# A Macaron block with an S4D layer: 14 other token orders in the square layers, and the last matrix moved by 64 bytes

## The reference

```python
def _L0_ffn_ref(x, w1_w, w1_s, w2_w, w2_s, h1_w, h1_s, h2_w, h2_s, w3_w, w3_s):
    h = jax.nn.silu(_tlin(x, w1_w, w1_s)) * _tlin(x, w2_w, w2_s)   # 256 -> 1024
    h = jax.nn.gelu(_tlin(h, h1_w, h1_s), approximate=False)       # 1024 -> 1024
    h = jax.nn.gelu(_tlin(h, h2_w, h2_s), approximate=False)       # 1024 -> 1024
    return _tlin(h, w3_w, w3_s)                                    # 1024 -> 256

x = x + 0.5 * _L0_ffn_ref(_layernorm(x, axis=-1), ...)
x = x + _L0_attn_ref(_layernorm(x, axis=-1), ...)    # FFT convolution with the S4D kernel, gelu, 256 x 256 projection
x = x + 0.5 * _L0_ffn_ref(_layernorm(x, axis=-1), ...)
```

## Time and profile before

| | |
|---|---|
| median of 2 runs | 1431.37 us (1431.02 to 1431.71) |
| the profiled execution, its own time | 1433.21 us |
| span of its trace, from the first to the last instruction | 1431.4 us |
| TensorE (PE) busy | 1423.7 us, 99% |
| VectorE (DVE) busy | 986.3 us, 69% |
| ScalarE (ACT) busy | 477.7 us, 33% |
| granted TensorE clock | 1.000 |

### The profile page before, as it was taken

One profiled execution on the slowest core, in us unless ns is written; L12 is line 12 of the kernel. 1 busy time (PEld: TensorE's weight loads), 2 busy tenths in 40 slices (PEclk: granted clock), 3 DMA queues, 4 the chain that ended last, 5 costly groups with the idle time before them and its releaser, 6 DMA issues.

```text
span 1431.4 us, 17284 instructions
## 1 busy us (share of the span) xinstructions
PE 1423.7 (99%) x6918; PEld 1166.7 (82%) x6918; DVE 986.3 (69%) x1736; ACT 477.7 (33%) x724; POOL 48.1 (3%) x42
## 2 busy tenths in 40 slices
PE   9999999999999999999999999999999999999998
PEld 4788888888878888788787888878878788888887
DVE  7867867775778887848878587784777754453433
ACT  5524342433425124232242332422424223141321
POOL 0000000000000000010000100001000010000000
PEclk9999999999999999999999999999999999999999
DMA  9000000011113211131210312112120212010000
GB/s 369 16 0 30 30 30 30 16 45 59 42 65 127 74 60 59 32 112 46 87 60 12 133 45 74 34 41 99 60 74 15 59 44 71 1 45 0 30 1 16
DMA packets 53906, 80.28 MB, mean 56 GB/s; under 512 B 2752, under 2 KB 45632, under 8 KB 52544
## 3 DMA queue, kind: packets, MB, share of 16 engines
q1 hardware_dynamic: 53824, 79.15, 16.3%
HBM read 57.12 MB, written 22.02 MB: 55 GB/s over the span
## 4 chain that ended last, share of the span: by engine, by line
PE 98%; DVE 1%; ACT 0%; issue 0%; POOL 0%
PE ps L1327 80%; PE ps L1403 8%; PE ps L1454 3%; PE ps L1507 2%; PE ps L1303 1%; PE ps L1449 1%; PE ps L1448 1%; PE ps L1416 1%; PE ps L1387 1%; PE ps L1497 0%; PE ps L1320 0%; PE ps L1389 0%; DVE hid_b_lo L1221 0%; PE ps L1431 0%; PE ps L1439 0%; DVE hid_b_hi L1219 0%
## 5 line engine op out<-in xcount | busy, mean ns | idle before, releaser
L503 ACT ACTIVATE act_o<-ps,scales 128x512 f32<-128x512 f32 x384 | 264.5, 690 | 897.1 <-PE ps L1327 895.3
L1327 PE MATMUL ps<-hid_b_hi,h 128*128 128x512 f32 x1024 | 401.5, 392 | 0.5 <-DVE hid_b_lo L1221 0.5
L1327 PE MATMUL ps<-hid_b_lo,h 128*128 128x512 f32 x1024 | 398.7, 389 | 0.0
L1327 PE MATMUL ps<-hid_a_hi,h 128*128 128x512 f32 x992 | 390.1, 393 | 0.1
L1327 PE MATMUL ps<-hid_a_lo,h 128*128 128x512 f32 x992 | 386.1, 389 | 0.0
L1327 PEld LDWEIGHTS ps<-hid_b_hi,h 128*128 128x128 f32 x1024 | 192.2, 188 | 42.1 <-issue 1.2
L1327 PEld LDWEIGHTS ps<-hid_b_lo,h 128*128 128x128 f32 x1024 | 192.2, 188 | 40.8 <-issue 1.2
L1327 PEld LDWEIGHTS ps<-hid_a_hi,h 128*128 128x128 f32 x992 | 186.2, 188 | 41.3 <-issue 2.2
L1327 PEld LDWEIGHTS ps<-hid_a_lo,h 128*128 128x128 f32 x992 | 186.2, 188 | 40.5 <-issue 2.2
L1327 PE MATMUL ps<-hid_b_hi,w 128*128 128x512 f32 x480 | 187.3, 390 | 0.1
L1327 PE MATMUL ps<-hid_b_lo,w 128*128 128x512 f32 x480 | 186.8, 389 | 0.0
(11 more groups left out here) (270 smaller groups left out, 1269.7 us busy)
## 6 DMA issues: line engine op xcount, KB each, us to landing
ks<-k_d SPq DMA_DIRECT2D x32, 512.0 KB, 3.8
raws<-in_weights SPq DMA_DIRECT2D x9, 1024.0 KB, 14.3
xin<-in_x SPq DMA_DIRECT2D x8, 512.0 KB, 3.7
x_d<-xin SPq DMA_DIRECT2D x8, 512.0 KB, 2.8
z_d<-xin SPq DMA_DIRECT2D x8, 512.0 KB, 2.8
zb<-z_d SPq DMA_DIRECT2D x8, 512.0 KB, 4.9
wb<-x_d SPq DMA_DIRECT2D x8, 512.0 KB, 4.1
x_d<-wb SPq DMA_DIRECT2D x8, 512.0 KB, 3.3
```

Of the source, the lines that this page charges most:

```text
L503: A(act_o[:, k % ACT_SLOTS], bank(source), func, scale=scale).then_inc(s_act, 1)
L1327: last = MM(o, weight[:, k, cols].bitcast(dt), part[:, k].bitcast(dt), start=(k == 0 and i == 0), stop=(k == n - 1 and i == len(act_) - 1))
```

## The change

Two things are changed.

First, `product` takes a function `order`, which for step k gives another view of the 512 tokens and of the 512 columns of the bank. `hidden` passes one that leaves step 0 as it is and uses the seven entries of ORDERS[1] for steps 1 to 7 in the first square layer, and those of ORDERS[2] in the second. `interleaved(runs, width)` cuts the 512 tokens into `runs` equal runs and takes `width` tokens of each run in turn, then the next `width` of each, and so on. The same view is put on the input and on the sums, so each token's sum still ends in its own column. The number of matmuls, columns and waits stays as it was. `interleaved(4, 128)` and `interleaved(2, 256)`, steps 6 and 7 of the second square layer, are the old order again. `hidden_ahead`, `layer_one` and `layer_three` are as before.

Second, w3 starts 128 bytes ahead of a multiple of LINE in place of 64. For that, scales goes from the front of the arena to the place behind w3, flag to the front, and expo to the zone at the end. Each matmul of `layer_three` reads the same 1024 bytes of w3 as before, 64 bytes further down.

```diff
--- before.py
+++ after.py
@@ -187,11 +187,11 @@
             return (*made, start)
 
 
-        scales, small, single, LAST = zone(0, ("scales", [P, 4, KH]), ("small", [P, N_SMALL]), ("single", [P, 4]))
-        LAST += (LINE - 64 - base - LAST) % LINE
+        small, single, flag, LAST = zone(0, ("small", [P, N_SMALL]), ("single", [P, 4]), ("flag", [P, 1], I32))
+        LAST += (LINE - 128 - base - LAST) % LINE
         w3, FRONT = zone(LAST, ("w3", [P, KH, D], F32R))
         raw_3, _ = zone(LAST, ("raw_3", [P, KH * D]))
-        flag, expo, FRONT = zone(FRONT, ("flag", [P, 1], I32), ("expo", [P, J]))
+        scales, FRONT = zone(FRONT, ("scales", [P, 4, KH]))
         assert (base + FRONT) % LINE == 0
         w1, w2, h1, h2, W0 = zone(FRONT, ("w1", [P, KD, HID], F32R), ("w2", [P, KD, HID], F32R),
                                   ("h1", [P, KH, HID], F32R), ("h2", [P, KH, HID], F32R))
@@ -212,10 +212,10 @@
         gated = gz[:, :, :].rearrange("p j d -> p (j d)").rearrange("p (m n) -> p m n", m=2)
         zhi, zlo = hid_b_hi[:, 0:KD], hid_b_lo[:, 0:KD]
 
-        zb, wb, fb, tt, ks, tables, stats, mv, vare, rstd, _ = zone(
+        zb, wb, fb, tt, ks, tables, stats, mv, vare, rstd, expo, _ = zone(
             Z0, ("zb", [P, 8, D]), ("wb", [P, 8, D]), ("fb", [P, 8, D]), ("tt", [P, 4, D]),
             ("ks", [P, 2, 4, D]), ("tables", [P, 6, P]), ("stats", [P, J, 6]), ("mv", [P, J, 2]), ("vare", [P, J]),
-            ("rstd", [P, J]))
+            ("rstd", [P, J]), ("expo", [P, J]))
         TAB0 = Z0 + 4 * D * (8 + 8 + 8 + 4 + 8)
         C2F, S2F, C2T, S2T, C4, S4 = range(6)
         ga = fb[:, :, :].rearrange("p u d -> p (u d)").rearrange("p (k t) -> p k t", k=KD)
@@ -1319,12 +1319,12 @@
                 for _ in range(WARM_UP):
                     MM(bank(7), act_o[:, 0, 0:P], act_o[:, 0], start=True, stop=True)
 
-            def product(o, weight, cols, act_, n, dt, after=None):
+            def product(o, weight, cols, act_, n, dt, after=None, order=lambda k, x: x):
                 for k in range(n):
                     if after:
                         after(k)
                     for i, part in enumerate(act_):
-                        last = MM(o, weight[:, k, cols].bitcast(dt), part[:, k].bitcast(dt),
+                        last = MM(order(k, o), weight[:, k, cols].bitcast(dt), order(k, part[:, k]).bitcast(dt),
                                   start=(k == 0 and i == 0), stop=(k == n - 1 and i == len(act_) - 1))
                 return last
 
@@ -1350,6 +1350,15 @@
                     pe.wait_ge(s_gate, at_gate(T, m - 2))
                 product(bank(o + 1), w2 if T else first(1), cols, z_parts, KD, dt).then_inc(s_u, 1)
 
+            def interleaved(runs, width):
+
+                return lambda x: x.rearrange("p (a b c) -> p b a c", a=runs, c=width)
+
+            ORDERS = {1: (interleaved(2, 2), interleaved(2, 4), interleaved(2, 8), interleaved(2, 16),
+                          interleaved(4, 16), interleaved(8, 16), interleaved(16, 16)),
+                      2: (interleaved(2, 32), interleaved(2, 64), interleaved(2, 128), interleaved(4, 32),
+                          interleaved(16, 2), interleaved(4, 128), interleaved(2, 256))}
+
             def of_hidden(k):
                 weight, source = (h1, (hid_a_hi, hid_a_lo)) if k < 2 * KH else (h2, (hid_b_hi, hid_b_lo))
                 return weight, slice(k % KH * P, (k % KH + 1) * P), source
@@ -1365,7 +1374,8 @@
                 if k == 2 * KH:
                     ready = lambda kk: pe.wait_ge(s_split, at_split(T, KH + kk))
                 weight, cols, source = of_hidden(k)
-                product(bank(k % 4), weight, cols, source, KH, dt, ready).then_inc(s_u, 1)
+                product(bank(k % 4), weight, cols, source, KH, dt, ready,
+                        lambda kk, x: ORDERS[k // KH][kk - 1](x) if kk else x).then_inc(s_u, 1)
 
             def sum_bits():
 
```

## The result

| | before | changed |
|---|---|---|
| median | 1431.37 us | 1551.23 us (1551.13 to 1551.33, 2 runs) |
| the profiled execution | 1433.21 us | 1551.13 us |
| span of its trace | 1431.4 us | 1549.3 us |

The ratio is 1.0837, with a 95% interval of 1.0791 to 1.0884: slower by 119.9 us. The forecast was 1535, the range 1427 to 1560.

The account below looks back on a forecast made before the run. The prediction took TensorE's streaming of 512 tokens per matmul as the bound. 103.7 us for the pairs, with 0 for wider orders, weight loads and last matrix, on 1431.4 gave 1535 us, range 1427 to 1560.

Parts of the forecast that it names:

- TensorE streams, so every change counts in full: Whole kernel: TensorE busy 1423.7 of 1431.4 us, so matmul time gained or lost shows one for one at the end.
- A pair costs a visit as in L1439: Square layers, (2,2) and (16,2): 504 matmuls at 432.5 in place of 226.75 ns, 103.7 us; bounds nothing and 109.6 us.
- The half record of float32: Half a plain float32 record takes 214.5 ns against float32r's 226.75, so float32 seems to read each element once for two cycles.
- Width 4 and more: Square layers, ten orders, 2512 matmuls: at most 128 jumps, 216 ns, lie under 226.75, so 0; ends -31 and +77 us.
- The weight loads: Square layers: new orders may meet stationary operand reads otherwise; 4.2 ns per matmul would lose 10.6 us; taken as 0.
- The last matrix: Layer three (L1403), w3 moved: all blocks fast wins 2.4 us, all slow loses 1.6; taken as 0.
- The chances: Slower by over 2%: 0.65; within 2%: 0.31; faster by over 2%: 0.04; own forecast 0.44; outside the range 0.18.
- R4: Square layers: alternating between runs is faster, ten orders gain 30.8 us; 1394 to 1401, or 1504 with doubled pairs; chance 0.07.
- R1: Square layers: a pair is free and every order runs as the old one; 1431 us; chance 0.28.
- R2: Square layers: a 0.38 ns stop at each change of 16-token block; 55.5 us more, 1487; chance 0.10.
- R3: Square layers: every jump adds its price, in SBUF reads or PSUM writes; 187 us more, 1618; chance 0.11.
- surplus of 12.25 ns: Old order in the square layers: a float32r matmul takes 226.75 ns, 12.25 above the 214.5 of half a float32 record.

Follow-up runs that it names:

- float32 orders: Kernel before, with plain float32 matmuls (L1454) reading in other orders: per record (16,2) 433 ns, (2,2) 454, (128,2) 468, (16,1) 843 to 864; old order 429.
- wide orders alone: Kernel before plus the change's orders without (2,2) and (16,2), w3 in its old place: 1462.56 us, ratio 1.0222.
- last survey: Kernel before, another read pattern in each square-layer unit, second layer's weights shifted 64 bytes: pairs of single-element streams 215.8 ns, 8 runs of singles 486.8.
- two_streams: Kernel before, square layers reading tokens 0, 256, 1, 257 and so on: 1393.59 us, ratio 0.9739; with layer_one (rounds 1 to 15) and layer three too: 1378.90 us, 0.9639.
- the surveys: Kernel before, one order or pattern per square-layer unit for all 8 steps; orders read and written 1826.2 us, read alone 1825.0, written alone 1432.8.
- survey of patterns: Kernel before, each square-layer unit reading its moving operand in a hand-built pattern, some repeating or overlapping: from 215.8 ns to 573.9 ns per matmul.
- pairs alone: Kernel before plus only (2,2) in step 1 of the first and (16,2) in step 5 of the second square layer: 1518.79 us, ratio 1.0616.

## Why the prediction was right or wrong

The time lay in the range, and the forecast was the nearest of the cases, 16 us below. That it came so near is in part luck, since two errors of opposite sign nearly cancel (below). Step by step:

- *TensorE streams, so every change counts in full.* Right. The sum of the distances gives 117.7 of 117.9 us, no wait was added.
- *A pair costs a visit as in L1439, 432.5 ns, for both orders: 103.7 us.* That a jump at every pair is paid by the read of the moving operand was right, and so was the size for (16,2), with 446 ns in the changed kernel and 56.2 us against 52.7. It was mis-sized for (2,2): 335 ns, 26.8 us against 51.0. The step took every jump as a visit to a new line. In (2,2) half of the visits return to a line with only one visit in between, and that is cheaper. L1439, which never returns soon, could not show it. And 1.69 ns per visited place, carried over from plain float32, is not how float32r pays in general: single elements from 16 runs take 434 ns for 512 visits, 0.85 each. For pairs the two come out alike.
- *The half record of float32 as the reason for the upper price.* Right: by the float32 orders, plain float32 takes (16,2) in the 433 ns that it needs anyway, where two sweeps in the manner of float32r would take about 880.
- *Width 4 and more: 0, since 216 ns of jumps lie under 226.75.* Wrong: 26.7 us in the changed kernel, 27.4 with the wide orders alone (31.9 with the matmuls beside them and the rest). This is the term that failed. It treated the two as alternatives of which the longer counts, but a jump comes on top: 7 to 24 ns per matmul in steady streams. The range held it (-31 to +77).
- *Neighbours.* Not in the sum. 5.9 us went into matmuls of the old order beside the new ones.
- *The weight loads: 0, up to 10.6.* With their place as it is, the runs show no share of them. Displaced by 64 bytes they cost the old order 6.8 ns and some of the wide orders 1 to 3.
- *The last matrix: -2.4 to +1.6, taken as 0.* +2.1 in the trace, +2.2 measured alone: just outside the bounds, since the new place brought a third kind of block (7.94), slower than the two that were known.
- The two errors that nearly cancel are -20.7 us for the pairs and +32.6 for the wide orders and their neighbours.
- *The chances.* R4 with doubled pairs, 1504, lies inside the range and would have been slower by over 2%, yet the sums of the chances put all of R4 outside the range, and within 2% or faster.

Of the rivals, R1 (a pair is free) and with it the Trainium skill's rule of two hits on a line of 16 bytes ("Advanced Engine Details and Errata", "Memory Cachelines") is out for a float32r stream if a pair is taken for the two hits. Counted for every second place, as the last survey suggests, it is near: two hits per line give 226.7, and one gives 430 to 490. R2's ladder was 313, 264, 239 for the first three orders; the trace has 335, 256, 243. There it is close, but it leaves (2,16) at 226.75, which has 240, and gives (2,2) and (16,2) the same price, while (16,2) costs twice (2,2)'s extra. R3 (each jump adds 0.85 ns, PSUM included) is out: PSUM pays nothing, and (2,4) had 29 ns and not 109. R4 said that alternating between runs removes the surplus of 12.25 ns. For all 12 orders of the change it is wrong. But the mechanism it names exists, with a width of 1, which the change did not have; I had argued that the surplus looks like a fixed rate, and that was wrong.

What is shown: where the price is paid, its size for each order, that for two streams reuse of a line and not distance makes (2,2) cheaper, and the time of two_streams. That there are two readers for even and odd places is a model that foretold the last survey; four fixed pairs 512 bytes apart (573.9 ns) and a fixed block of 64 bytes (241.3 ns), which it does not foretell, stay open. So does why a jump costs what it does at widths of 4 and more, which is measured but not explained. Open too is why (8,2) is slower than (16,2).

## What to carry to other kernels

When TensorE streams float32r operands at a granted clock of 1.0, look at the distance between starts: 226.7 ns for 512 neighbouring columns is not the floor, and reading two single-element streams in turn (two halves, or just two neighbouring lines of 16 bytes) gives 215.8. The permutation can be undone where PSUM is read with a step of two columns, or in the layout of a constant matrix, both of which cost nothing here. Don't let a float32r stream jump at every pair in SBUF, which cost 100 to 260 ns per matmul in the surveys; in PSUM it may. And before a mean of distances is read, look at the granted clock of its stretch.

## What the runs showed of the hardware that was not expected

- Single elements from 2 runs: 215.8 ns; from 4: 283.3; from 8: 486.8; from 16: 434.2. Pairs from 2 runs, 340.0, cost more than single elements from 2 or 4.
- Reads and writes of a matmul can have different orders, and only the reads matter. With 15 orders of width 2 and more in the writing, one in each unit, the kernel took 1432.8 us in all.
- TensorE's granted clock can fall while the engine is busy without a gap: in every round of the survey of patterns it fell to 1.2 GHz in the unit of four fixed pairs, whose matmuls are 574 ns apart. That distance was the same at either level.
- A place of the stationary operand 64 bytes further on costs the old order 6.8 ns in 226.7, and a stream in two single runs nothing.
- Four of VectorE's 128 subtractions into hid_a_lo (L1221) became very long in the kernels with (16,2) in the second square layer. By shape, ns min/median/max, in the changed kernel; then from its timeline one of them, and the GpSimd (POOL) work that began 0.22 us before it:

```profile
L1221 DVE TENSOR_TENSOR hid_a_lo<-act_o,hid_a_hi x128: 691/693/2768, 74.3 to 1537.8; 128x512 fp32r<-128x512 f32 x128
```

```profile
656.76 5.22 POOL L475 TENSOR_TENSOR wb<-wb,tt 128x1024 f32<-128x1024 f32 x2 [32.53 <-DMA wb<-x_d]
656.98 2.77 DVE L1221 TENSOR_TENSOR hid_a_lo<-act_o,hid_a_hi 128x512 fp32r<-128x512 f32 x1
```

2768 ns at most against 696 before, with the same median; the kernel with the pairs alone has 2884. All four, in both kernels, start while the first of GpSimd's two instructions of L475 runs, and end 0.55 us after it does. No other subtraction of the 128 starts there. With the wide orders alone the four that meet L475 began 0.6 us ahead of it and keep 693 ns. In the trace of the kernel before none meets it, but two casts (L1219) that begin during L475 take 923 and 906 ns in place of 427. So the long ones go with GpSimd's work and not with what TensorE reads: the change only moved them under it. How the one holds up the other is not shown. It cost no time here.
